# Eight experts of one layer: loop written out, the next expert's transposes ahead of the last product, rows added at evacuation, the inner norm derived from the outer

## The chip, the cores and the metric

The kernel runs on one core of a Trainium2 chip. The metric is the device time of one execution in microseconds (us). TensorE (PE) does the matrix products and the transposes, VectorE (DVE) and ScalarE (ACT) read its results out of PSUM, GpSimd (POOL) does small things in SBUF, and SyncE (SP) issues the DMA transfers. The profile keeps TensorE's weight loads (PEld) apart from its matmuls (PE); they overlap, and since every matmul here has a weight load of its own, the start of a weight load shows when its matmul could be issued.

## The reference

A four-layer network over x of 16 x 256 x 256 (f32). Each layer adds a gated attention and a gated feed-forward part. The change lies in the feed-forward part of the third layer (index 2), which gets the layer norm of x and not x itself:

```python
def _layernorm(x, axis=-1, eps=1e-05): ...          # the outer norm, ahead of every part
def _L2_ffn_ref(x, ln_g, ln_b, attn_w, attn_b, gate_w, w1, b1, w2, b2, next_w, next_b):
    ...
    x_attn = _layernorm(x_flat, ln_g, ln_b) @ attn_w + attn_b + x_flat   # a second, inner norm
    ...
    g = x_attn.reshape(MICRO_BATCHES, E, tpe, Dx)                        # 2 x 8 x 256 x 256
    h = gelu(einsum('metd,edf->metf', g, w1) + b1)                       # 256 -> 1024
    y = einsum('metf,efd->metd', h, w2) + b2                             # 1024 -> 256
    out = gelu(y @ next_w + next_b)
    return out
x = x + tanh(g_ffn[2]) * _L2_ffn_ref(_layernorm(x), ...)
```

Expert e works on batch rows e and e + 8, whatever the gate says.

## The kernel before

The program is a row of stages with a barrier between them; `layer2_experts` is the eighth of nine. It runs eight experts one after the other. Each expert has two halves u = 0, 1 (batches e and e + 8, 256 rows each), and P = 128, C = 2, D = 256. A half has four PSUM banks of its own: A, H0, H1 and Y. For one half the work is:

- **front**: VectorE takes statistics of x (`ln_stats`), GpSimd makes the reciprocal root (`ln_rstd`: an add and a power), VectorE writes the outer norm `xn` (`ln_apply`); then the same three steps on `xn` give the inner norm `nn`. TensorE transposes `nn` into bank A (`transpose4`, four transposes), ScalarE reads that with gain and bias into `n2T`.
- **attention product** (wa): `n2T` by `wa` into A; the rows `xn` themselves are added in the same accumulation, by eight products of 128 columns of `xn` with the identity over both halves (line 2627). ScalarE reads A with the bias `ba` into `xaT` (line 2587).
- **h**: `xaT` by `w1`, four groups a half that go to H0 and H1 in turn; ScalarE's Gelu into `hT` (line 2594).
- **y**: `hT` by `w2` into Y, then VectorE adds `b2` into `yT` (line 2557).
- **z**: `yT` by `wn` into A again; VectorE adds `bn` (line 2562), ScalarE's Gelu, VectorE adds the result times the gate to x (line 2567).

TensorE's order in one expert is wa for both halves, h, y, z, and last the transposes of the next expert (`front(e + 1)`). VectorE makes the next expert's front between its two `yT`: the half u = 0 is read, then the whole front, then u = 1. Those orders are written by hand; the engines meet through counting semaphores. The experts stand in a hardware loop of three rounds with two experts each (`passes`), and the last two experts are written out behind it.

SP's queue loads weights of 2 MB for an expert in two sets of buffers; the set of expert e + 2 is sent for when both `yT` of expert e are read. The first expert's set and `wa`, `wn`, `bn` and the small columns are sent for when the stage begins.

An f32 product of the program is two rows in the profile (64 rows of h an expert for 32 products), a transpose is one.

Of the kernel before, what the change touches and what calls it, by code (L numbers as in the profile page):

```python
# [2454 lines left out]
def layer2_experts(nc, env, w, sem_):  # L2455

    E, F = 8, 1024
    FC = F // P  # L2460
    with ExitStack() as ctx:
# [5 lines left out]
        xn, nn, n2T, xaT, yT, z = (sb(n, [P, 2, C, D]) for n in ("xn", "nn", "n2T", "xaT", "yT", "z"))  # L2467
        hT = sb("hT", [P, 2, FC, S])
        st, mv, rstd = sb("st", [P, 2, C, 6]), sb("mv", [P, 2, C, 2]), sb("rstd", [P, 2, C])
        e_in = [sem_(f"e2_in{k}") for k in range(2)]  # L2470
        (w_in, st_rdy, rstd_rdy, nn_rdy, nT_mm, nT_rdy, xa_mm, xa_rdy, h_mm, h_rdy, y_mm, y_rdy, z_mm, z_rdy, zg_rdy,
         v_ch, f_ch, g_ch) = (
            sem_("e2_" + n) for n in ("w_in", "st_rdy", "rstd_rdy", "nn_rdy", "nT_mm", "nT_rdy", "xa_mm", "xa_rdy",
                                      "h_mm", "h_rdy", "y_mm", "y_rdy", "z_mm", "z_rdy", "zg_rdy", "v_ch", "f_ch",
                                      "g_ch"))

        A, H0, H1, Y = ([env.bank(4 * u + j) for u in (0, 1)] for j in range(4))
        gain_in, a_in = (sem_("e2_" + n) for n in ("gain_in", "wa_in"))
        loads = 2
        block = ctx.enter_context(nc.Block())  # L2480

        def experts(eng, body):

            def two(i, more):
                body(2 * i, True, 0)
                body(2 * i + 1, more, 1)
            passes(eng, two, E // 2)

        @block.sync
        def _(sp):  # L2490
# [7 lines left out]
            def load(e, k):
                at = bass.ds(e, 1)
                sp.dma_start(w1[:, k], w["L2_ffn_w1"][at].rearrange("e (k p) f -> p (e k) f", p=P)).then_inc(e_in[k], 16)  # L2500
                sp.dma_start(w2[:, k], w["L2_ffn_w2"][at].rearrange("e (k p) f -> p (e k) f", p=P)).then_inc(e_in[k], 16)
                sp.dma_start(b1[:, k], b1v[at].rearrange("e p f -> p (e f)")).then_inc(e_in[k], 16)
                sp.dma_start(b2[:, k], b2v[at].rearrange("e p f -> p (e f)")).then_inc(e_in[k], 16)

            load(0, 0)
            load_weight(sp, wn[:], w["L2_ffn_next_w"], w_in)
            sp.dma_start(bn[:], rows(w["L2_ffn_next_b"])).then_inc(w_in, 16)
            load(1, 1)
            with sp.Fori(1, E // 2) as i:
                for k in range(2):  # L2510

                    sp.wait_ge(y_rdy, 4 * i + 2 * k - 2)
                    load(2 * i + k, k)

        @block.gpsimd
        def _(g):
            ch = Chain(g, g_ch)

            def front(e):
                ch.start(4 * e)  # L2520
                for n in range(4):
                    u = n % 2
                    g.wait_ge(st_rdy, 4 * e + n + 1)
                    ln_rstd(g, ch, mv[:, u], rstd[:, u], env.mhalf, env.eps5).then_inc(rstd_rdy, 1)
            front(0)

            def body(e, more, k):
                if more:
                    front(e + 1)
            experts(g, body)  # L2530

        @block.vector
        def _(v):
            ch, fch = Chain(v, v_ch), Chain(v, f_ch)

            def front(e):
                fch.start(6 * e)
                for u in (0, 1):
                    ln_stats(v, fch, env.x[:, e + E * u], st[:, u], mv[:, u], env.scrap).then_inc(st_rdy, 1)
                for u in (0, 1):  # L2540
                    v.wait_ge(rstd_rdy, 4 * e + u + 1)
                    fch.link(ln_apply(v, xn[:, u], env.x[:, e + E * u], mv[:, u], rstd[:, u]))
                    ln_stats(v, fch, xn[:, u], st[:, u], mv[:, u], env.scrap).then_inc(st_rdy, 1)
                for u in (0, 1):
                    v.wait_ge(rstd_rdy, 4 * e + u + 3)
                    ln_apply(v, nn[:, u], xn[:, u], mv[:, u], rstd[:, u]).then_inc(nn_rdy, 1)

            front(0)
            v.wait_ge(w_in, 16 * loads)

            def body(e, more, k):
                for u in (0, 1):
                    if u == 1 and more:
                        front(e + 1)
                    v.wait_ge(y_mm, nth(e, u))
                    for c in range(C):
                        last = v.tensor_scalar(yT[:, u, c], Y[u][:, c], b2[:, k, c:c + 1], None, ALU.add)  # L2557
                    last.then_inc(y_rdy, 1)
                for u in (0, 1):
                    v.wait_ge(z_mm, nth(e, u))  # L2560
                    for c in range(C):
                        last = v.tensor_tensor(z[:, u, c], A[u][:, c], bn[:], ALU.add)
                    last.then_inc(z_rdy, 1)
                for u in (0, 1):
                    v.wait_ge(zg_rdy, nth(e, u))
                    b = e + E * u
                    v.scalar_tensor_tensor(env.x[:, b], z[:, u], env.tg[:, 6:7], env.x[:, b], ALU.mult, ALU.add)
            experts(v, body)

        @block.scalar  # L2570
        def _(a):
            def front(e):
                for u in (0, 1):
                    a.wait_ge(nT_mm, nth(e, u))
                    for c in range(C):
                        last = a.activation(n2T[:, u, c], A[u][:, c], ACT.Identity, scale=gain[:, c:c + 1],
                                            bias=bias[:, c:c + 1])
                    last.then_inc(nT_rdy, 1)
# [3 lines left out]

            def body(e, more, k):
                for u in (0, 1):
                    a.wait_ge(xa_mm, nth(e, u))
                    for c in range(C):
                        last = a.activation(xaT[:, u, c], A[u][:, c], ACT.Identity, bias=ba[:, c:c + 1])
                    last.then_inc(xa_rdy, 1)
                for q in range(FC // C):
                    for u in (0, 1):  # L2590
                        a.wait_ge(h_mm, 8 * e + 2 * q + u + 1)
                        for c in range(C):
                            f = C * q + c
                            last = a.activation(hT[:, u, f], (H0, H1)[q % 2][u][:, c], ACT.Gelu, bias=b1[:, k, f:f + 1])
                        last.then_inc(h_rdy, 1)
                for u in (0, 1):
                    a.wait_ge(z_rdy, nth(e, u))
                    a.activation(z[:, u], z[:, u], ACT.Gelu).then_inc(zg_rdy, 1)
                if more:
                    front(e + 1)  # L2600
            experts(a, body)

        @block.tensor
        def _(pe):
            def front(e):
                for u in (0, 1):
                    pe.wait_ge(nn_rdy, nth(e, u))

                    if not (isinstance(e, int) and e == 0):
                        pe.wait_ge(z_rdy, nth(e - 1, u))  # L2610
                    transpose4(pe, A[u], nn[:, u], env.ident[:]).then_inc(nT_mm, 1)
# [3 lines left out]

            def body(e, more, k):

                pe.wait_ge(e_in[k], 32 * (e - k) + 64)
                for u in (0, 1):
                    pe.wait_ge(nT_rdy, nth(e, u))  # L2620
                    for m in range(C):
                        for kk in range(C):
                            pe.matmul(A[u][:, m], wa[:, kk, chunk(m)], n2T[:, u, kk], start=(kk == 0), stop=False,
                                      skip_group_check=True)
# [4 lines left out]
                    last.then_inc(xa_mm, 1)  # L2629
                for q in range(FC // C):  # L2630
                    for u in (0, 1):
                        if q == 0:
                            pe.wait_ge(xa_rdy, nth(e, u))
                        if q >= 2:

                            pe.wait_ge(h_rdy, 8 * e + 2 * (q - 2) + u + 1)
                        for c in range(C):
                            for kk in range(C):
                                last = pe.matmul((H0, H1)[q % 2][u][:, c], w1[:, k, kk, chunk(C * q + c)],
                                                 xaT[:, u, kk], start=(kk == 0), stop=(kk == C - 1))  # L2640
                        last.then_inc(h_mm, 1)
                for u in (0, 1):
                    pe.wait_ge(h_rdy, 8 * e + 6 + u + 1)
                    product(pe, lambda m: Y[u][:, m], lambda f, m: w2[:, k, f, chunk(m)], lambda f: hT[:, u, f],
                            K=FC).then_inc(y_mm, 1)
                pe.wait_ge(w_in, 16 * loads)
                for u in (0, 1):
                    pe.wait_ge(y_rdy, nth(e, u))
                    product(pe, lambda m: A[u][:, m], lambda kk, m: yT[:, u, kk, chunk(m)],
                            lambda kk: wn[:, kk]).then_inc(z_mm, 1)  # L2650
                if more:
                    front(e + 1)
            experts(pe, body)

# [786 lines left out]
```

## Time and profile before

| | us |
|---|---|
| runs of the kernel before | 2900.1, 2896.9, 2907.57 (median 2900.1) |
| the profiled execution | 2907.57, its span 2905.7 |
| TensorE matmul busy | 2682.1 (92%) |
| VectorE busy | 1584.7 (55%) |
| ScalarE busy | 1292.9 (44%) |
| GpSimd busy | 709.2 (24%) |
| this stage, first statistics to the last row added | 2044.35 to 2376.04, so 331.7 (11%) |

The mean granted clock of TensorE is 0.959 of its full speed. "Granted clock 1.00" is the level of 2.4 GHz, 0.50 that of 1.2 GHz. The profiled execution is the slowest of the three, 7.5 us above the median.

### The profile page before, as it was taken

How to read it: one execution, taken by the hardware profiler on the slowest of the kernel's cores; microseconds unless marked ns; L12 is line 12 of the kernel's file. 1: busy time of each engine (PE TensorE's matmuls, PEld its weight loads, DVE VectorE, ACT ScalarE, POOL GpSimd, SP SyncE). 2: the span in 40 equal slices, each digit the busy share in tenths (PEclk: the TensorE clock that was granted, in tenths of full speed). 3: DMA queues.
4: the chain of work that ended last, by engine and by line, in shares of the span. 5: the costliest groups of instructions: out<-in, count | busy, mean ns of one | idle time of the engine just before them, and what ended most of it. 6: DMA issues, size and time to landing. Idle time of an engine off the chain costs nothing. (4 is left out here: it accounts for less than half of the span.)

```text
span 2905.7 us, 64340 instructions
## 1 busy us (share of the span) xinstructions
PE 2682.1 (92%) x24765; PEld 2044.8 (70%) x24766; DVE 1584.7 (55%) x4380; ACT 1292.9 (44%) x2444; POOL 709.2 (24%) x1095
## 2 busy tenths in 40 slices
PE   7979999999997998997989589999799989969998
PEld 5855555555555887886878455555688878859998
DVE  4747777777771113887766367776232238751111
ACT  1236777676762212553426356665233324532221
POOL 1202333233221000111646423230111015551111
PEclk9999999999997999998899789999899999979999
DMA  9710000000003443931125300100211120035553
GB/s 321 293 35 3 3 3 3 3 3 3 3 3 114 147 157 124 358 126 61 61 81 163 123 24 26 33 18 3 97 53 34 58 81 1 23 133 178 179 180 118
DMA packets 136290, 249.29 MB, mean 86 GB/s; under 512 B 26716, under 2 KB 86364, under 8 KB 129632
## 3 DMA queue, kind: packets, MB, share of 16 engines
q1 hardware_dynamic: 114608, 185.11, 19.1%
q10 hardware_dynamic: 11536, 35.28, 3.1%
q0 software_dynamic: 9888, 25.38, 2.4%
q8 instruction: 172, 2.82, 0.4%
q14 instruction: 86, 0.70, 0.1%
HBM read 148.75 MB, written 97.75 MB: 85 GB/s over the span
## 5 line engine op out<-in xcount | busy, mean ns | idle before, releaser
L532 DVE TENSOR_REDUCE m0hnm<-banks 128x4 f32<-128x1024 f32 x256 | 313.5, 1225 | 157.1 <-PE banks L482 157.1
L553 ACT ACTIVATE m0hpT<-banks 128x1024 f32<-128x1024 f32 x256 | 262.3, 1025 | 181.8 <-PE banks L496 181.6
L482 PE MATMUL banks<-m0hk,m0hq 32*128 32x256 f32 x2048 | 290.6, 401 | 9.5 <-DVE m0hnm L532 8.4
L496 PE MATMUL banks<-m0hq,m0hk 32*128 32x256 f32 x2048 | 291.7, 401 | 1.4 <-ACT m0hpT L553 1.4
L482 PEld LDWEIGHTS banks<-m0hk,m0hq 32*128 32x128 f32 x2048 | 175.2, 184 | 98.4 <-DVE m0hnm L532 89.9
L556 ACT ACTIVATE a2hpT<-banks,A2low 128x512 f32<-128x512 f32 x256 | 162.1, 684 | 128.7 <-PE banks L496 128.7
L532 DVE TENSOR_REDUCE a2hnm<-banks 128x4 f32<-128x1024 f32 x128 | 156.8, 1225 | 99.4 <-PE banks L482 99.3
L496 PEld LDWEIGHTS banks<-m0hq,m0hk 32*128 32x128 f32 x2048 | 182.0, 185 | 3.4 <-issue 1.6
L482 PE MATMUL banks<-a2hk,a2hq 32*128 32x256 f32 x1024 | 148.2, 407 | 9.5 <-DVE a2hnm L532 8.2
L496 PE MATMUL banks<-a2hq,a2hk 32*128 32x256 f32 x1024 | 148.2, 406 | 1.9 <-ACT a2hpT L556 1.9
L3275 PEld LDWEIGHTS banks<-E3xT,E3w 128*128 128x128 f32 x1248 | 146.6, 193 | 2.4 <-DVE E3xT L3199 0.5
L3275 PE MATMUL banks<-E3xT,E3w 128*128 128x128 f32 x1248 | 147.0, 277 | 0.1
L599 POOL TENSOR_TENSOR m0hnrm<-m0hraw,m0hrec 128x256 f32<-128x256 f32 x64 | 39.8, 622 | 436.1 <-DVE m0hrec L594 436.1
L3241 ACT ACTIVATE E3hT<-banks 128x512 f32<-128x512 f32 x78 | 46.6, 598 | 220.8 <-PE banks L3275 212.4
L3286 PE MATMUL banks<-wide_all,E3hT 128*128 x624 | 141.0, 379 | 0.0
L509 PE MATMUL banks<-m0hpT,m0hv 128*32 128x256 f32 x2048 | 136.6, 385 | 1.1 <-ACT m0hpT L553 1.1
L1263 DVE SCALAR_TENSOR_TENSOR x_all<-banks,pick_w,x_all 128x512 f32 (+1 forms) x32 | 24.0, 751 | 206.8 <-PE banks L1226 206.8
L482 PEld LDWEIGHTS banks<-a2hk,a2hq 32*128 32x128 f32 x1024 | 90.0, 187 | 65.1 <-DVE a2hnm L532 49.7
L2557 DVE TENSOR_SCALAR E2yT<-banks,E2b 128x256 f32<-128x256 f32 x32 | 14.0, 477 | 223.2 <-PE banks L61 223.2
L1218 PE MATMUL banks<-wide_all,E0w 128*128 (+1 forms) x512 | 117.3, 383 | 9.8 <-DMA E0w<-in_L_ffn_fw_dram 9.8
L3286 PEld LDWEIGHTS banks<-wide_all,E3hT 128*128 128x128 f32 x624 | 115.6, 190 | 14.2
L1226 PE MATMUL banks<-E0w,E0hT 128*128 128x256 f32 x512 | 115.6, 379 | 0.0
(493 smaller groups left out, 6157.4 us busy)
## 6 DMA issues: line engine op xcount, KB each, us to landing
E3w<-in_L_ffn_W_dram SPq DMA_DIRECT2D x39, 1024.0 KB, 4.8
slots<-A0pad SPq DMA_DIRECT2D x8, 4290.0 KB, 33.7
slots_x<-A1pad ACTq DMA_DIRECT2D x8, 4290.0 KB, 13.8
E0w<-in_L_ffn_fw_dram SPq DMA_DIRECT2D x64, 512.0 KB
E2w<-in_L_ffn_w_dram SPq DMA_DIRECT2D x16, 1024.0 KB
E1xin<-slots SPq DMA_DIRECT2D x71, 130.0 KB
m0hq<-m0hnmT SPq DMA_DIRECT2D x512, 1.0 KB
A2routed<-routed SPq DMA_DIRECT2D x16, 512.0 KB, 3.8
```

Source lines behind the costliest of these rows:

```text
L482: ins = pe.matmul(self.scores[:, j, tc], self.q[self.strip(half, j), u, e, c, chunk(tc)], self.k[self.strip(half, j), u, e, c], start=True ...
L496: ins = pe.matmul(self.turned[:, j, kc], self.k[self.strip(half, j), u, e, c, chunk(kc)], self.q[self.strip(half, j), u, e, c], start=True ...
L509: ins = pe.matmul(self.out[32 * g:32 * g + 32, e], self.v[:, u, kc, 8 * c + 2 * g + e], self.pT[:, e, g, kc], start=(kc == 0), stop=(kc == ...
L532: v.tensor_reduce(self.nm[:, n % 2, :, 16 * half:16 * half + 9:8].rearrange("p c g -> p g c"), self.scores, AX.X, ALU.max, negate=True).th ...
L553: ins = a.activation(dst, self.turned, ACT.Exp)
L556: ins = a.activation(dst[:, :, kc], self.turned[:, :, kc], ACT.Exp, bias=self.low[:, n // 4, kc:kc + 1])
L599: g.tensor_tensor(self.nrm[:].rearrange("p s e k -> p e s k"), self.raw[:, :, :, 0:KD], self.rec[:].unsqueeze(3).broadcast_to([P, 2, 8, KD ...
L1218: last = pe.matmul(env.bank(4 * (j % 2) + half)[:, m], w1[:, j, k, chunk(f)], env.n2T[:, 2 * i + j // 2, k], start=(k == 0), stop=(k == C ...
L1226: last = pe.matmul(env.bank(4 * (j % 2) + 2)[:, tc], hT[:, j % 2, k, chunk(tc)], w2[:, j, k], start=(k == 0), stop=(k == FC - 1))
L3241: a.activation(hT[:, u, 4 * q:4 * q + 4], hidden_bank(u, q), ACT.Gelu).then_inc(h_free, 1)
L3275: last = pe.matmul(hidden_bank(u, q)[:, c], w1[:, u, k, chunk(4 * q + c)], xT[:, u, k], start=(k == 0), stop=(k == C - 1))
L3286: last = pe.matmul(bank(6 + u)[:, 0], hT[:, u, f], w2[:, e, f].rearrange("p e d -> p (e d)"), start=(f == 0), stop=(f == FC - 1))
```

## The change

Only `layer2_experts` changes. The loop is gone: the eight experts are written out for all engines. The semaphores are counted with constants.

```diff
         @block.gpsimd
...
-            def front(e):
-                ch.start(4 * e)
-                for n in range(4):
-                    u = n % 2
-                    g.wait_ge(st_rdy, 4 * e + n + 1)
-                    ln_rstd(g, ch, mv[:, u], rstd[:, u], env.mhalf, env.eps5).then_inc(rstd_rdy, 1)
...
+            for e in range(E):
+                for u in (0, 1):
+                    g.wait_ge(st_rdy, 2 * e + u + 1)
+                    g.tensor_scalar(var[:, u, 1], mv[:, u, :, 1], 1.0 + 1e-5, 1e-10, ALU.mult, ALU.add)
+                    ch.link(g.tensor_tensor(var[:, u, 0], mv[:, u, :, 1], env.eps5[:], ALU.add))
+                    g.tensor_tensor(root[:, u].rearrange("p t c -> p (t c)"), var[:, u].rearrange("p t c -> p (t c)"),
+                                    env.mhalf[:, 0:2 * C], ALU.pow).then_inc(rstd_rdy, 1)
         @block.vector
...
+                for u in (0, 1):
+                    v.wait_ge(rstd_rdy, 2 * e + u + 1)
...
+                    for t, dst in ((0, xn), (1, nn)):
+                        for c in range(C):
+                            ins = v.tensor_scalar(dst[:, u, c, :], env.x[:, e + E * u, c, :], mv[:, u, c, 0:1],
+                                                  root[:, u, t, c:c + 1], ALU.subtract, ALU.mult)
+                    ins.then_inc(nn_rdy, 1)
...
-                for u in (0, 1):
-                    if u == 1 and more:
-                        front(e + 1)
-                    v.wait_ge(y_mm, nth(e, u))
...
+            for e in range(E):
+                for u in (0, 1):
+                    v.wait_ge(xa_mm, 2 * e + u + 1)
+                    v.tensor_tensor(xaT[:, u], A[u], xT[:, u], ALU.add).then_inc(xa_rdy, 1)
+                if e:
+                    residual(e - 1)
+                if e + 1 < E:
+                    front(e + 1)
+                for u in (0, 1):
+                    v.wait_ge(y_mm, 2 * e + u + 1)
...
         @block.scalar
...
+                    for c in range(C):
+                        a.activation(n2T[:, u, c], H0[u][:, c], ACT.Identity, scale=gain[:, c:c + 1], bias=bias[:, c:c + 1])
+                    for c in range(C):
+                        ins = a.activation(xT[:, u, c], H1[u][:, c], ACT.Identity, bias=ba[:, c:c + 1])
+                    ins.then_inc(nT_rdy, 1)
...
         @block.tensor
...
-                    transpose4(pe, A[u], nn[:, u], env.ident[:]).then_inc(nT_mm, 1)
+                    transpose4(pe, H0[u], nn[:, u], env.ident[:])
+                    transpose4(pe, H1[u], xn[:, u], env.ident[:]).then_inc(nT_mm, 1)
...
-                pe.wait_ge(e_in[k], 32 * (e - k) + 64)
...
-                        for tc in range(C):
-
-                            last = pe.matmul(A[u][:, m, chunk(tc)], xn[:, u, tc, chunk(m)], env.ident[:],
-                                             start=False, stop=True, skip_group_check=True)
...
+                    pe.wait_ge(nT_rdy, 2 * e + u + 1)
+                    if e:
+                        pe.wait_ge(z_rdy, 2 * e - 2 + u + 1)
+                    product(pe, lambda m: A[u][:, m], lambda kk, m: wa[:, kk, chunk(m)], lambda kk: n2T[:, u, kk])\
+                        .then_inc(xa_mm, 1)
+                pe.wait_ge(e_in[k], 64 * (e // 2 + 1))
...
+                if e + 1 < E:
+                    front(e + 1)
                 pe.wait_ge(w_in, 16 * loads)
```

In words: the inner norm is no longer taken from statistics of `xn`; its root is worked out from the variance of x, and `nn` is written straight from x beside `xn`. The rows `xn` are transposed too, read by ScalarE with the bias into a new tile `xT`, and added by VectorE when it reads the attention product. The transposes go to H0 and H1 and not to A. The wait for the expert's own weights stands ahead of h and no longer ahead of wa. VectorE makes the next front ahead of both `yT`, behind the reading of the attention product and the former expert's last addition to x.

TensorE's order of one expert before, where it is written out behind the loop (E2nn and E2xn are the two norms, E2n2T the transposed inner norm, E2xaT, E2hT and E2yT the inputs of h, y and z):

```order
L77 MATMUL banks<-ident,E2nn 128x128 x8
L2623 MATMUL banks<-E2n2T,E2wa 128x256 x2
L2627 MATMUL banks<-ident,E2xn 128x128 x2
L2623 MATMUL banks<-E2n2T,E2wa 128x256 x2
...
L2639 MATMUL banks<-E2xaT,E2w 128x256 x32
L61 MATMUL banks<-E2hT,E2w 128x256 x32
L61 MATMUL banks<-E2wn,E2yT 128x256 x8
```

The same stretch of TensorE's order in the changed kernel, from the wa of one expert to that of the next:

```order
L61 MATMUL banks<-E2n2T,E2wa 128x256 x8
L61 MATMUL banks<-E2xaT,E2w 128x256 x32
L61 MATMUL banks<-E2hT,E2w 128x256 x32
L77 MATMUL banks<-ident,E2nn 128x128 x4
L77 MATMUL banks<-ident,E2xn 128x128 x4
L77 MATMUL banks<-ident,E2nn 128x128 x4
L77 MATMUL banks<-ident,E2xn 128x128 x4
L61 MATMUL banks<-E2wn,E2yT 128x256 x8
L61 MATMUL banks<-E2n2T,E2wa 128x256 x8
```

The sixteen transposes stand between y and z, and the products with the identity are gone. On VectorE the order of one expert before, from the first `yT` to the addition to x (written out behind the loop; E2st and E2mv are the statistics):

```order
L2557 TENSOR_SCALAR E2yT<-banks,E2b 128x256 x2
L84 BN_STATS E2st<-x_all 128x6 x2
...
L101 TENSOR_SCALAR E2xn<-x_all,E2mv,E2rstd 128x256 x2
L84 BN_STATS E2st<-E2xn 128x6 x2
...
L101 TENSOR_SCALAR E2nn<-E2xn,E2mv,E2rstd 128x256 x4
L2557 TENSOR_SCALAR E2yT<-banks,E2b 128x256 x2
L2562 TENSOR_TENSOR E2z<-banks,E2bn 128x256 x4
L2567 SCALAR_TENSOR_TENSOR x_all<-E2z,tg,x_all 128x512 x2
```

VectorE in the changed kernel, one expert in the middle:

```order
L2550 TENSOR_TENSOR E2xaT<-banks,E2xT 128x512 x2
L2544 SCALAR_TENSOR_TENSOR x_all<-E2z,tg,x_all 128x512 x2
L2524 BN_STATS E2st<-x_all 128x6 x2
...
L2536 TENSOR_SCALAR E2xn<-x_all,E2mv,E2root 128x256 x2
L2536 TENSOR_SCALAR E2nn<-x_all,E2mv,E2root 128x256 x2
...
L2558 TENSOR_SCALAR E2yT<-banks,E2b 128x256 x4
L2565 TENSOR_TENSOR E2z<-banks,E2bn 128x256 x4
```

The front stands ahead of the pair of `yT` and no longer inside it, and the reading of the attention product, ScalarE's before, is VectorE's.

## Rows read from the trace of the kernel before

The stretches of rows 1 and 7 give length, then busy time (and instructions) of PE, PEld, DVE, ACT and POOL, then the granted clock, the DMA engines' busy share and GB/s.

**Rows 1.** Stretches by engine: steady experts, then the stage's opening.
```profile
2063.05:2342.44 279.39, 265.29 (x1291) 230.59 (x1289) 76.84 (x266) 86.77 (x187) 26.87 (x56) 1.00 0.14 45
2044.30:2063.05 18.75, 10.33 (x40) 8.51 (x40) 6.58 (x28) 4.16 (x7) 3.85 (x8) 0.56 0.76 261
```

**Rows 2.** What weight loads waited for, 2063 to 2376: us, times, longest.
```profile
PEld banks L61 <- DVE E2yT L2557: 7.0, 7, 1.0
PEld banks L2623 <- issue: 5.8, 5, 1.2
PEld banks L77 <- issue: 5.0, 7, 0.7
PEld banks L2623 <- ACT E2n2T L2576: 2.2, 2, 1.1
```

**Rows 3.** Weight loads in time: start, us, line, names [idle before, releaser]; several experts.
```profile
2097.75 0.73 PEld L2623 LDWEIGHTS banks<-E2n2T,E2wa 128*128 128x128 f32 x4 [1.15 <-issue]
...
2102.98 13.69 PEld L2639 LDWEIGHTS banks<-E2xaT,E2w 128*128 128x128 f32 x64
...
2130.51 1.70 PEld L61 LDWEIGHTS banks<-E2wn,E2yT 128*128 128x128 f32 x8
2133.20 1.59 PEld L61 LDWEIGHTS banks<-E2wn,E2yT 128*128 128x128 f32 x8 [0.99 <-DVE E2yT L2557]
2134.82 0.57 PEld L77 LDWEIGHTS banks<-ident,E2nn 128*128 128x128 f32 x4
2136.11 0.42 PEld L77 LDWEIGHTS banks<-ident,E2nn 128*128 128x128 f32 x4 [0.71 <-issue]
2137.61 0.73 PEld L2623 LDWEIGHTS banks<-E2n2T,E2wa 128*128 128x128 f32 x4 [1.09 <-ACT E2n2T L2576]
...
2337.21 0.73 PEld L2623 LDWEIGHTS banks<-E2n2T,E2wa 128*128 128x128 f32 x4 [1.15 <-issue]
```

**Rows 4.** VectorE and ScalarE in time, the turn from expert 1 to 2.
```profile
2124.01 0.88 DVE L2557 TENSOR_SCALAR E2yT<-banks,E2b 128x256 f32<-128x256 f32 x2 [26.38 <-PE banks L61]
2124.81 0.74 DVE L84 BATCH_NORM_STATS2 E2st<-x_all 128x6 f32 x2
...
2132.28 0.87 DVE L2557 TENSOR_SCALAR E2yT<-banks,E2b 128x256 f32<-128x256 f32 x2
...
2135.24 0.76 DVE L2562 TENSOR_TENSOR E2z<-banks,E2bn 128x256 f32<-128x256 f32 x2 [1.42 <-PE banks L61]
...
2136.56 1.92 ACT L2576 ACTIVATE E2n2T<-banks,E2bias,E2gain 128x256 f32<-128x256 f32 x4
```

**Rows 5.** Groups by line and form: out<-in xcount | busy us, mean ns | idle.
```profile
L2962 DVE TENSOR_TENSOR A3on<-banks,A3den 128x512 f32<-128x512 f32 x16 | 11.0, 688 | 3.6 <-PE banks L3065 2.6 <-issue 0.8
L2587 ACT ACTIVATE E2xaT<-banks,E2ba 128x256 f32<-128x256 f32 x32 | 13.4, 471 | 31.7 <-PE banks L2627 31.7
L101 DVE TENSOR_SCALAR E2nn<-E2xn,E2mv,E2rstd 128x256 f32<-128x256 f32 x32 | 11.5, 402 | 4.7 <-POOL E2rstd L96 4.7
L722 POOL TENSOR_TENSOR M0root<-M0var,mhalf 128x4 f32<-128x4 f32 x16 | 16.5, 1033 | 1.2
L720 POOL TENSOR_SCALAR M0var<-M0mv 128x2 f32<-128x2 f32 x16 | 3.1, 193 | 14.8 <-DVE M0mv L782 14.6
```

**Rows 6.** All engines in time, the stage's opening.
```profile
2044.35 0.75 DVE L84 BATCH_NORM_STATS2 E2st<-x_all 128x6 f32<-128x256 f32 x2 [1.31 <-PEq L3348]
...
2050.66 0.72 PEld L77 LDWEIGHTS banks<-ident,E2nn 128*128 128x128 f32 x4 [9.37 <-DVE E2nn L101]
...
2054.95 2.07 PE L2623 MATMUL banks<-E2n2T,E2wa 128*128 128x256 f32 x4 [1.85 <-DMA E2b<-in_L_ffn_b_dram]
```

**Rows 7.** Short stretches: the clock's rise here and in the next stage.
```profile
2060.50:2061.00 0.50, 0.50 (x3) 0.38 (x3) 0.00 (x0) 0.50 (x2) 0.00 (x0) 0.64 1.09 320
2385.00:2386.00 1.00, 1.00 (x5) 0.85 (x5) 0.35 (x2) 0.00 (x0) 0.92 (x2) 0.94 0.64 205
```

**Rows 8.** The next stage's first product on TensorE, in time.
```profile
2382.03 3.06 PEld L61 LDWEIGHTS banks<-A3wq,a3xnT 128*128 128x128 f32 x8 [1.15 <-issue]
```

More of the change, by code:

```diff
@@ L2496, in _, with load @@
             b2v = w["L2_ffn_b2"].rearrange("p (e c) -> e p c", e=E)
[L2498 to L2505, printed above, removed]
+            def load(e):
+                k = e % 2
+                sp.dma_start(w1[:, k], w["L2_ffn_w1"][e].rearrange("(k p) f -> p k f", p=P)).then_inc(e_in[k], 16)
+                sp.dma_start(w2[:, k], w["L2_ffn_w2"][e].rearrange("(k p) f -> p k f", p=P)).then_inc(e_in[k], 16)
+                sp.dma_start(b1[:, k], b1v[e]).then_inc(e_in[k], 16)
+                sp.dma_start(b2[:, k], b2v[e]).then_inc(e_in[k], 16)
+            load(0)
             load_weight(sp, wn[:], w["L2_ffn_next_w"], w_in)
             sp.dma_start(bn[:], rows(w["L2_ffn_next_b"])).then_inc(w_in, 16)
[L2508 to L2513, printed above, removed]
+            load(1)
+            for e in range(2, E):
+                sp.wait_ge(y_rdy, 2 * e - 2)
+                load(e)
         @block.gpsimd
@@ L2556, in body @@
                     for c in range(C):
-                        last = v.tensor_scalar(yT[:, u, c], Y[u][:, c], b2[:, k, c:c + 1], None, ALU.add)
-                    last.then_inc(y_rdy, 1)
+                        ins = v.tensor_scalar(yT[:, u, c], Y[u][:, c], b2[:, e % 2, c:c + 1], None, ALU.add)
+                    ins.then_inc(y_rdy, 1)
+                if e == 0:
+                    v.wait_ge(w_in, 16 * loads)
                 for u in (0, 1):
-                    v.wait_ge(z_mm, nth(e, u))
+                    v.wait_ge(z_mm, 2 * e + u + 1)
@@ L2561, in body @@
                     for c in range(C):
-                        last = v.tensor_tensor(z[:, u, c], A[u][:, c], bn[:], ALU.add)
-                    last.then_inc(z_rdy, 1)
-                for u in (0, 1):
[L2565 to L2568, printed above, removed]
+                        ins = v.tensor_tensor(z[:, u, c], A[u][:, c], bn[:], ALU.add)
@@ L2570, in _ @@
+                    ins.then_inc(z_rdy, 1)
+            residual(E - 1)
         @block.scalar
@@ L2573, in front @@
                 for u in (0, 1):
-                    a.wait_ge(nT_mm, nth(e, u))
+                    a.wait_ge(nT_mm, 2 * e + u + 1)
                     for c in range(C):
-                        last = a.activation(n2T[:, u, c], A[u][:, c], ACT.Identity, scale=gain[:, c:c + 1],
-                                            bias=bias[:, c:c + 1])
-                    last.then_inc(nT_rdy, 1)
+                        a.activation(n2T[:, u, c], H0[u][:, c], ACT.Identity, scale=gain[:, c:c + 1], bias=bias[:, c:c + 1])
+                    for c in range(C):
+                        ins = a.activation(xT[:, u, c], H1[u][:, c], ACT.Identity, bias=ba[:, c:c + 1])
+                    ins.then_inc(nT_rdy, 1)
             a.wait_ge(gain_in, 16 * 3)
             front(0)
[L2583 to L2588, printed above, removed]
+            a.wait_ge(e_in[0], 64)
+            for e in range(E):
+                if e:
+                    a.wait_ge(e_in[e % 2], 64 * (e // 2 + 1))
                 for q in range(FC // C):
@@ L2593, in body @@
                             f = C * q + c
-                            last = a.activation(hT[:, u, f], (H0, H1)[q % 2][u][:, c], ACT.Gelu, bias=b1[:, k, f:f + 1])
-                        last.then_inc(h_rdy, 1)
+                            ins = a.activation(hT[:, u, f], (H0, H1)[q % 2][u][:, c], ACT.Gelu, bias=b1[:, e % 2, f:f + 1])
+                        ins.then_inc(h_rdy, 1)
+                if e + 1 < E:
+                    front(e + 1)
                 for u in (0, 1):
-                    a.wait_ge(z_rdy, nth(e, u))
+                    a.wait_ge(z_rdy, 2 * e + u + 1)
                     a.activation(z[:, u], z[:, u], ACT.Gelu).then_inc(zg_rdy, 1)
-                if more:
-                    front(e + 1)
-            experts(a, body)
         @block.tensor
@@ L2632, in body @@
                         if q == 0:
-                            pe.wait_ge(xa_rdy, nth(e, u))
+                            pe.wait_ge(xa_rdy, 2 * e + u + 1)
                         if q >= 2:
                             pe.wait_ge(h_rdy, 8 * e + 2 * (q - 2) + u + 1)
[L2637 to L2641, printed above, removed]
+                        product(pe, lambda m: (H0, H1)[q % 2][u][:, m], lambda kk, m: w1[:, k, kk, chunk(C * q + m)],
+                                lambda kk: xaT[:, u, kk]).then_inc(h_mm, 1)
                 for u in (0, 1):
@@ L2645, in body @@
                             K=FC).then_inc(y_mm, 1)
+                if e + 1 < E:
+                    front(e + 1)
                 pe.wait_ge(w_in, 16 * loads)
                 for u in (0, 1):
[L2648 to L2653, printed above, removed]
+                    pe.wait_ge(y_rdy, 2 * e + u + 1)
+                    product(pe, lambda m: A[u][:, m], lambda kk, m: yT[:, u, kk, chunk(m)], lambda kk: wn[:, kk])\
+                        .then_inc(z_mm, 1)
 def layer3(nc, env, w, sem_):
```

59 lines of the change are left out of this document (23 added, 36 removed).

## The prediction

> **What bounds the kernel now.** I looked first at busy time by stretches. In the steady experts TensorE's matmuls are busy 265.3 of 279.4 us at a granted clock of 1.00, VectorE and ScalarE under a third [rows 1]: the stage is TensorE's, and only what TensorE does or waits for counts. The opening is another regime, 18.75 us at a mean clock of 0.56 [rows 1].
>
> Then the waits of the weight loads. They sat idle 7.0 us for the second `yT`, 8.0 us (5.8 + 2.2) ahead of wa and 5.0 us ahead of the second half's transposes [rows 2]. That is 20.0 us over seven turns from one expert to the next, 2.86 each. The waits called "issue" are the same waits as the named one: they stand at the same places with the same length [rows 3].
>
> Then the turn in time. From wa of expert 1 (2097.75) to wa of expert 7 (2337.21) are six turns, so a turn is 239.46 / 6 = 39.91 us [rows 3]. Inside it h and y take 2130.51 - 2102.98 = 27.53 us for 128 rows, 0.215 us each. z and wa have 16 rows each, 3.44 us. From wa's start to h's start are 2102.98 - 2097.75 = 5.23 us, so the identity products take 5.23 - 3.44 = 1.79 us. What is left for the eight transposes is 39.91 - 27.53 - 3.44 - 5.23 - 2.86 = 0.85 us, 0.106 each; the four that directly follow z spread over 0.57 us, 0.143 each [rows 3], which I keep as an upper bound.
>
> Last, why it waits. VectorE reads `yT` of half 0 at 2124.01, starts the front at 2124.81 and reads half 1 only at 2132.28, 7.47 us later, though y had ended by 2130.51 [rows 3, 4]. So the second z starts late, and the transposes, which share bank A with z, wait for VectorE to read that z at 2135.24; then wa waits for ScalarE's reading of the transposes, from 2136.56 on [rows 3, 4]. Three engines pass one thing round with TensorE empty in between.
>
> **The change, part by part.**
>
> *Order of the turn.* The transposes need nothing of z now, and the front is long done when y ends. After y TensorE has 16 transposes, 1.70 us, then z, 3.44 us, then wa. I put y's end at 0 and count an engine's start 0.45 us after the last weight load of its product (the second z's loads end at 2133.20 + 1.59 = 2134.79, VectorE starts at 2135.24) [rows 3, 4]. Second `yT`: ready at 0.45 + 0.87 = 1.3, needed at 1.7 + 1.7 = 3.4. ScalarE's four readings of a half take 2 x 0.48 + 2 x 0.47 = 1.9 us [rows 4, 5]; half 0 is ready at 0.85 + 0.45 + 1.9 = 3.2 and half 1 at 5.1, needed at 5.1 and 6.9. The second z is read 0.45 + 0.76 = 1.2 us after its last load, and wa's second half comes 1.72 later: 0.5 us to spare. All three waits go, 2.86 us a turn.
>
> *Rows added at evacuation.* The identity products go: 1.79 us a turn. Eight transposes come: 0.85 (up to 1.14). VectorE's addition of 128x512 from PSUM is not in this trace; the nearest rows are 0.69 us for such a product of two operands and 0.76 for a pair of additions with the same number of elements [rows 4, 5]. Each half is ready 1.14 to 1.21 us after its wa and h of that half comes 1.72 after it. It costs nothing, with 0.5 us of cover; were the cover gone, all of h would wait for it and each further us would be a us a turn.
>
> *Inner norm from the variance.* VectorE loses two statistics a turn. GpSimd's power over 128x4 takes 1.03 us and the extra scalar step 0.19, as the same trick does elsewhere in this kernel [rows 5]; both lie in the front. That now runs during h: behind the second addition and the two updates of x. Even at its old 7.47 us plus some 3 us ahead of it, it ends 11 us into h and y's 27.5. VectorE's new wait there, for the former expert's Gelu, holds the front and through it the transposes; it has more than 15 us of cover. Nothing in the steady turn.
>
> *Weights.* The wait for an expert's weights stands later, the transfers are sent for a little earlier in the turn, since `yT` is read earlier. No cost, no gain in the turn.
>
> *Loop written out.* The turn into expert 2 crosses the loop's end and wa waits 1.09 us there; the turn into expert 7 lies in straight code, 1.15 [rows 3]. So the branch costs nothing today. The Trainium skill (Runtime: NRT & Kernel Launch, Instruction fetch mechanics) says that a taken branch out of the prefetched pages stalls for a fetch, by which written-out code would gain more than my sum; the trace does not show it here.
>
> So a turn saves 2.86 + 1.79 - 0.85 = 3.80 us (3.5 with the dear transposes, all sixteen at 0.143: 3.2), and seven turns 26.6 (22.4).
>
> *Opening.* Before: statistics from 2044.35, first transposes at 2050.66, first product at 2054.95, held for the last small weight of expert 0 [rows 6]. After: two statistics (0.95 with their aggregation, by the 0.75 of the row and an estimate of 0.2), GpSimd 0.19 + 0.19 + 1.03 with small gaps, 1.5, four applications at 0.40 [rows 5, 6]: transposes at about 2048.5. Eight of them at the half clock, 0.18 to 0.21 us each by the 0.72 us of four [rows 6], 0.45 for the hand-over, four readings: first wa at about 2052.7, without the wait for the weights. Those arrive at 2054.95 and h needs them later. The clock was full 2060.86 - 2054.95 = 5.9 us after the first product (the 0.64 of that half us puts the step at 2060.86) [rows 6, 7], and in the next stage 2385.12 - 2382.03 = 3.1 us after it [rows 7, 8]. wa then ends, and h starts, between 2057.8 and 2059.1, at the latest 2059.6 if all of wa runs at half speed (16 rows at 0.43). Before, h started where wa's 16 + 16 rows ended, 27.53 + 7.15 us (z 3.44, transposes 0.85, idle 2.86) ahead of the next expert's wa at 2097.75: 2063.07. I take 2058.6, so 4.5 us saved (3.5 to 5.3).
>
> **Sum.** 26.6 + 4.5 = 31.1 us. The stage's end is as before: the last expert has no next front, and y, z and the additions to x follow each other as they did. On the profiled execution 2907.6 - 31.1 = 2876.5. That one is 7.5 us above the median of its three runs, and nothing says this stage is why; against the median, 2900.1 - 31.1 = 2869.
>
> **The rivals.**
>
> *New waits take part of it.* Two hand-overs have only 0.5 us of cover: z read before wa, and the sums before h. If VectorE's two steps are each 1 to 1.5 us longer than their rows, each costs 0.5 to 1 us, so 1 to 2 us a turn and 7 to 14 us in all: 2876 to 2883. Against it: both are VectorE alone, which is otherwise idle at that time. 12 in 100.
>
> *The clock drops in the turn: slower.* Sixteen transposes stand in a row where products with full columns stood nearby before. If the granted clock falls to 0.50 there and stays low through transposes, z and wa, those 8.6 us become 17.2, 60 us in seven turns, net 29 slower: 2929. It decides from 4.4 us lost per turn, half of that stretch. Against it: TensorE was emptier in today's turn (2.86 us idle and eight transposes) and kept 1.00 throughout [rows 1, 2]. The Trainium skill speaks for this rival (TensorE: Matmul & The Clock Gate, PE-mode transpose): there the full clock does not engage for transposes. The trace agrees for the opening, where eight transposes alone left it at the lower level, and does not in the turn. 4 in 100.
>
> *The change does not do what it says.* The stage gets shorter and the next one gives it back, because its start waits for something else. Its first work is VectorE's statistics of x, which follow this stage's last addition, so I see nothing else: 4 in 100, about 2900.
>
> *More.* The turn saves the same, the opening 7 or more and the next stage's clock rises earlier: 35 to 40, 2860 to 2865; 6 in 100.
>
> **How the numbers follow.** The forecast holds 74 in 100: 2869, with 27 to 33 us saved, and some 4 us either way for the spread of single runs (2896.9 to 2907.6): 2863 to 2877. The range reaches into the first rival and the last one: 2861 to 2882. A measurement of this kernel can tell about 0.5%, 14.5 us, from no change. The forecast, "more" and nearly all of "new waits" lie beyond it: 0.91 faster; 0.05 the same; 0.04 slower.
>
> **What would show it.** In the profile after: a turn of 36.1 us from wa to wa; no idle row of weight loads between y and the next h; sixteen transposes in about 1.7 us; h of expert 0 starting 14 to 15 us into the stage instead of 18.7; a granted clock of 1.00 from there to the last z. I am wrong if weight loads still wait on VectorE's sums or on z, if the transposes take over 0.15 us each, or if the clock dips in the turn.

## The result, and the profile after

The changed kernel takes 2864.1 us (median of 4 runs), the kernel before 2901.1 beside it: ratio 0.9878, interval 0.9858 to 0.9898. A second measurement gave 2867.6 us (6 runs) against 2898.4 (10 runs): 0.9887, interval 0.9863 to 0.9911. So the change saves 36.9 us by the first, 30.7 by the second. The profiled execution took 2864.39 us with a span of 2862.2.

A cleaner measure is the stage itself, from its first statistics of x to the next stage's first statistics: 332.64 us before, 300.78 after, so **31.9 us**. Both intervals hold it (29.6 to 41.2 us, and 25.8 to 39.7). Of the two executions of experiment 6 below, one took 9042.8 us, more than three times any other, and is left out.

Stretches of the profile after, with columns as in [rows 1]; the first answers to the steady experts there, the second to the opening, the last two to [rows 7]:

```profile
2043.88:2319.00 275.12, 275.12 (x1331) 243.32 (x1330) 74.30 (x212) 87.47 (x199) 19.65 (x42) 1.00 0.16 53
2031.71:2043.88 12.17, 7.72 (x32) 6.71 (x33) 5.33 (x19) 3.39 (x8) 2.82 (x6) 0.61 0.84 255
2041.00:2041.50 0.50, 0.50 (x3) 0.39 (x2) 0.00 (x0) 0.33 (x1) 0.00 (x0) 0.68 1.16 307
2041.50:2042.00 0.50, 0.50 (x4) 0.45 (x3) 0.00 (x0) 0.00 (x0) 0.00 (x0) 1.00 1.21 297
```

TensorE's matmuls are busy all of the steady stretch where 14 us were empty before, and the opening is 12.2 us long and not 18.7. What weight loads waited for in the whole stage (2031 to 2333), as in [rows 2], is two waits of the opening and no more:

```profile
PEld banks L77 <- DVE E2nn L2536: 7.2, 1, 7.2
PEld banks L61 <- issue: 0.7, 1, 0.7
```

A turn in time, weight loads, VectorE and ScalarE (they answer to [rows 3, 4]; L77 transposes, L61 is every product, L2558 yT, L2565 z, L2550 the new addition):

```profile
2057.69 13.79 PEld L61 LDWEIGHTS banks<-E2hT,E2w 128*128 128x128 f32 x64
2071.50 0.57 PEld L77 LDWEIGHTS banks<-ident,E2nn 128*128 128x128 f32 x4
2072.05 0.47 PEld L77 LDWEIGHTS banks<-ident,E2xn 128*128 128x128 f32 x4
...
2073.36 3.32 PEld L61 LDWEIGHTS banks<-E2wn,E2yT 128*128 128x128 f32 x16
2076.71 3.43 PEld L61 LDWEIGHTS banks<-E2n2T,E2wa 128*128 128x128 f32 x16
...
2071.92 0.88 DVE L2558 TENSOR_SCALAR E2yT<-banks,E2b 128x256 f32<-128x256 f32 x2 [6.03 <-PE banks L61]
2075.47 0.76 DVE L2565 TENSOR_TENSOR E2z<-banks,E2bn 128x256 f32<-128x256 f32 x2 [2.67 <-PE banks L61]
2077.12 0.76 DVE L2565 TENSOR_TENSOR E2z<-banks,E2bn 128x256 f32<-128x256 f32 x2 [0.90 <-PE banks L61]
2078.85 0.69 DVE L2550 TENSOR_TENSOR E2xaT<-banks,E2xT 128x512 f32<-128x512 f32 x1 [0.97 <-PE banks L61]
2080.57 0.69 DVE L2550 TENSOR_TENSOR E2xaT<-banks,E2xT 128x512 f32<-128x512 f32 x1 [1.04 <-PE banks L61]
...
2072.79 1.02 ACT L2575 ACTIVATE E2n2T<-banks,E2bias,E2gain 128x256 f32<-128x256 f32 x2 [13.85 <-PE banks L77]
```

From one h to the next (2043.88 to 2080.16) are 36.28 us: h 13.81, y 13.81, sixteen transposes 1.86 (2071.50 to 2073.36), z 3.35, wa 3.45. No weight load carries an idle time any more; it is VectorE and ScalarE that wait for TensorE. Seven turns are alike to 0.01 us.

The opening in time (answers to [rows 6]; the power's price to [rows 5]):

```profile
2031.71 0.75 DVE L2524 BATCH_NORM_STATS2 E2st<-x_all 128x6 f32<-128x256 f32 x2 [1.29 <-PEq L3330]
2033.37 1.02 POOL L2512 TENSOR_TENSOR E2root<-E2var,mhalf 128x4 f32<-128x4 f32 x1
2035.86 0.71 PEld L77 LDWEIGHTS banks<-ident,E2nn 128*128 128x128 f32 x4 [7.21 <-DVE E2nn L2536]
2039.80 4.05 PEld L61 LDWEIGHTS banks<-E2n2T,E2wa 128*128 128x128 f32 x16 [0.66 <-issue]
2043.88 2.13 PEld L61 LDWEIGHTS banks<-E2xaT,E2w 128*128 128x128 f32 x10
2332.49 0.75 DVE L203 BATCH_NORM_STATS2 a3st<-x_all 128x6 f32<-128x256 f32 x2 [0.94 <-PEq L3330]
```

Transposes 4.15 us into the stage, wa at 8.09, h at 12.17. The clock is full from 2041.32 (the 0.68 of its half us), 1.5 us after the first product. The last row is the next stage's start; from there to the end of the span are 529.7 us, 528.7 before; the twelve profiles, whatever the kernel, have 528.6 to 530.8 there, so no giving back shows.

### The profile page after: what moved, and what is told of

It reads as the page before. It is cut to its first block and busy times, and to the rows that moved or that the text cites. A ratio compares the mean times of both kernels' runs of the same rounds, so it can differ in the third digit from the quotient of the medians.

```text
span 2862.2 us, 63825 instructions
## 1 busy us (share of the span) xinstructions
PE 2660.0 (93%) x24701; PEld 2032.0 (71%) x24702; DVE 1580.4 (55%) x4316; ACT 1285.0 (45%) x2439; POOL 701.0 (24%) x1079
## 5 line engine op out<-in xcount | busy, mean ns | idle before, releaser
L1249 ACT ACTIVATE E0hT<-banks 128x512 f32<-128x512 f32 x64 | 34.7, 594 | 179.3 <-PE banks L1218 179.3
```

## The experiments

Each kernel's stage in its profile, and its time. Opening: stage's start to the first weight load of h; turn: h to h.

| kernel | stage | opening | turn | median | ratio to before, interval |
|---|---|---|---|---|---|
| before | 332.64 | 18.70 | 39.87 to 39.93 | 2901.1 | |
| 1 loop written out | 332.74 | 18.55 | 39.93 to 40.01 | 2898.0 | 0.9999, 0.9983 to 1.0016 |
| 2 and the order | 313.65 | 18.73 | 37.20 | 2877.5 | 0.9916, 0.9896 to 0.9937 |
| 4 changed, statistics of the rows | 302.22 | 13.60 | 36.28 | 2866.5 | 0.9885, 0.9866 to 0.9904 |
| changed | 300.78 | 12.17 | 36.28 | 2864.1 | 0.9878, 0.9858 to 0.9898 |
| 3 changed, transposes behind z | 309.38 | 12.16 | 37.51 | 2879.3 | 0.9934, 0.9911 to 0.9958 |
| 5 changed, front between yT | 301.07 | 12.46 | 36.28 | 2863.9 | 0.9867, 0.9847 to 0.9887 |
| 6 changed, transposes twice | 315.03 | 14.20 | 38.03 | one run, 2882.5 | |
| 7 changed, addition twice | 301.05 | 12.53 | 36.28 | 2870.1 | 0.9888, 0.9868 to 0.9908 |
| 8 changed, products ahead | 299.16 | 10.55 | 36.28 | 2862.0 | 0.9860, 0.9843 to 0.9876 |
| 9 changed, again | 300.84 | 12.23 | 36.28 | 2867.6 | 0.9887, 0.9863 to 0.9911 |
| 10 before, again | 332.61 | 18.67 | 39.86 to 39.94 | 2900.4 | |

The stage of one kernel repeats to 0.06 us (9 and 10), the whole kernel to some ten us, so most verdicts below rest on the stage. Differences of 0.3 us between kernels are not to be read as an effect: in 5 and 7 the clock rose 0.6 us later than in the changed kernel, at 10.2 us into the stage and not 9.6, and 0.6 us more at half speed is 0.3 us of work.

**1. The loop written out, alone** (kernel before; SP's loop of loads, not shown, too).

```diff
-            def two(i, more):
-                body(2 * i, True, 0)
-                body(2 * i + 1, more, 1)
-            passes(eng, two, E // 2)
+            for e in range(E):
+                body(e, e + 1 < E, e % 2)
...
```

> The kernel before with its loop of experts written out and nothing else. Lengths of the stage are from its first statistics to the first statistics of the next stage: 332.6 us before, 300.8 after. My theory: the loop cost nothing, since the turn over the loop's end was as long as one in straight code; stage 332.6 us, turn 39.9, time as before within 5 us. Rival, written-out code is what pays: a stage of 325 us or less.

Turn and stage stay. The waits of [rows 3] are all there in straight code, the third of them 1.16 where it was 1.09 at the loop's end:

```profile
2122.11 1.59 PEld L61 LDWEIGHTS banks<-E2wn,E2yT 128*128 128x128 f32 x8 [1.00 <-DVE E2yT L2553]
...
2125.01 0.42 PEld L77 LDWEIGHTS banks<-ident,E2nn 128*128 128x128 f32 x4 [0.71 <-issue]
2126.59 0.73 PEld L2619 LDWEIGHTS banks<-E2n2T,E2wa 128*128 128x128 f32 x4 [1.16 <-issue]
```

The loop cost nothing: 0.9999. The Trainium skill (Runtime: NRT & Kernel Launch, Instruction fetch mechanics) says that a taken branch to code outside the prefetched pages stalls; no run here shows such a stall.

**2. The order, on top of 1.** Transposes go to H0, `front(e + 1)` stands ahead of z on TensorE and ahead of both yT on VectorE, and ScalarE reads the transposes ahead of its last Gelu; identity products and statistics of the rows stay.

```diff
+                if more:
+                    v.wait_ge(xa_mm, 2 * e + 2)
+                    front(e + 1)
                 for u in (0, 1):
-                    if u == 1 and more:
-                        front(e + 1)
...
-                    transpose4(pe, A[u], nn[:, u], env.ident[:]).then_inc(nT_mm, 1)
+                    transpose4(pe, H0[u], nn[:, u], env.ident[:]).then_inc(nT_mm, 1)
...
+                if more:
+                    front(e + 1)
                 pe.wait_ge(w_in, 16 * loads)
...
```

> The kernel before, written out, with the order of the turn alone: transposes (eight, of the inner norm only) into the other bank and ahead of the last product, VectorE's front ahead of both readings of y, ScalarE's reading of the transposes ahead of its last Gelu. Rows still added by products with the identity, inner norm still from statistics, the wait for the weights still ahead of the attention product. My theory: the order gives the three waits of a turn, 2.8 us: turn 37.1, stage 332.6 - 7 x 2.8 = 313 us, opening as before (18.7 us). Rival, the order needs the shorter front or the added rows to pay: a turn of 38.5 or more, stage 323 or more.

The turn falls by 2.71 us, the stage by 19.1: the three waits (2.86 by the weight loads' idle time), of which none is left in the turns, and 60% of the whole gain. The opening is untouched, its first product still waits and then runs at half speed until 16.6 us into the stage (the 0.83 of its quarter us). Weight loads in time, the last two rows one turn apart, then that stretch:

```profile
2043.64 0.71 PEld L77 LDWEIGHTS banks<-ident,E2nn 128*128 128x128 f32 x4 [0.60 <-DVE E2nn L101]
2046.58 1.35 PEld L2619 LDWEIGHTS banks<-E2n2T,E2wa 128*128 128x128 f32 x4 [2.22 <-issue]
...
2054.74 5.27 PEld L2635 LDWEIGHTS banks<-E2xaT,E2w 128*128 128x128 f32 x25
...
2091.93 12.17 PEld L2635 LDWEIGHTS banks<-E2xaT,E2w 128*128 128x128 f32 x57
```

```profile
2052.51:2052.76 0.25, 0.25 (x2) 0.21 (x2) 0.00 (x0) 0.25 (x2) 0.00 (x0) 0.83 0.93 240
```

**3. The changed kernel with the transposes behind z again.**

```diff
-                if e + 1 < E:
-                    front(e + 1)
                 pe.wait_ge(w_in, 16 * loads)
...
+                if e + 1 < E:
+                    front(e + 1)
```

> The changed kernel with the sixteen transposes put back behind the last product; all else as changed. My theory: the attention product must then wait for ScalarE to read the first half's transposes (0.45 + 1.9 us after eight of them, while the other eight take 0.93): about 1.4 to 1.6 us more a turn, turn 37.8, stage 311 to 312 us. Rival, with other banks and an early front the place no longer matters: stage 301.

The direction is right, the size a little less: 1.23 us a turn. One wait came back, ahead of wa for ScalarE's reading of the transposes, in all seven turns:

```profile
PEld banks L61 <- ACT E2xT L2577: 8.4, 7, 1.2
```

So the place ahead of z is worth 8.6 us of the stage even with the front early and A kept free. z is the work that covers ScalarE.

**4. The changed kernel with the inner norm from statistics of the rows**, as before the change.

```diff
-                    ch.link(g.tensor_tensor(var[:, u, 0], mv[:, u, :, 1], env.eps5[:], ALU.add))
...
+                    ln_rstd(g, ch, mv[:, u], rstd[:, u], env.mhalf, env.eps5).then_inc(rstd_rdy, 1)
...
+                    fch.link(ln_apply(v, xn[:, u], env.x[:, e + E * u], mv[:, u], rstd[:, u]))
+                    ln_stats(v, fch, xn[:, u], st[:, u], mv[:, u], env.scrap).then_inc(st_rdy, 1)
...
+                    ln_apply(v, nn[:, u], xn[:, u], mv[:, u], rstd[:, u]).then_inc(nn_rdy, 1)
```

> The changed kernel with the inner norm taken again from statistics of the outer one. My theory: the front is hidden under the products, so the turn stays at 36.3 us and only the opening grows, by 2 to 2.5 us; stage 303 us. Rival, the shorter front is what lets the transposes come early: a turn longer by 1 us or more, stage 310 or more.

Nothing in the turn, 1.4 us in the opening where 2 to 2.5 were expected (1.1 against the 12.46 of experiment 5, whose clock rose later). The transposes begin 2.17 us later, but part of that is won back: the clock is full before the first product is issued, so wa takes 3.34 us and not 4.08. Weight loads in time, then stretches of half a us:

```profile
2040.52 0.71 PEld L77 LDWEIGHTS banks<-ident,E2nn 128*128 128x128 f32 x4 [9.37 <-DVE E2nn L101]
...
2042.92 0.87 PEld L77 LDWEIGHTS banks<-ident,E2xn 128*128 128x128 f32 x4
2044.46 3.32 PEld L61 LDWEIGHTS banks<-E2n2T,E2wa 128*128 128x128 f32 x16 [0.67 <-issue]
2047.80 2.35 PEld L61 LDWEIGHTS banks<-E2xaT,E2w 128*128 128x128 f32 x11
```

```profile
2043.50:2044.00 0.50, 0.50 (x4) 0.29 (x2) 0.00 (x0) 0.50 (x3) 0.00 (x0) 0.52 1.19 303
2044.00:2044.50 0.50, 0.17 (x2) 0.04 (x1) 0.00 (x0) 0.50 (x2) 0.00 (x0) 1.00 1.08 318
```

What TensorE did in this stage before the clock rose (at about 2044, 3.5 us after the first weight load) is sixteen transposes in a row and nothing else.

**5. The changed kernel with VectorE's front between the two yT again.**

```diff
-                if e + 1 < E:
-                    front(e + 1)
                 for u in (0, 1):
+                    if u == 1 and e + 1 < E:
+                        front(e + 1)
```

> The changed kernel with VectorE's next front put back between the two readings of y; transposes still ahead of the last product. In the changed kernel the front takes 5.7 us and its first half is ready 4.1 us after it starts. My theory: it starts about 5.6 us before y ends, so both halves are ready when TensorE comes to them, and the second reading of y has the transposes and half the last product as cover; turn 36.3 to 36.6 us, stage 301 to 303. Rival, the early front is what removed the wait for the second reading of y: turn 37 or more, stage 306 or more.

The turn is the same, and the 0.3 us of the stage are the clock's later rise in the opening (the last row below). The shorter front ends just ahead of the second y, VectorE then waits 0.40 us and reads yT as early as before:

```profile
2062.16 0.88 DVE L2558 TENSOR_SCALAR E2yT<-banks,E2b 128x256 f32<-128x256 f32 x2 [20.03 <-PE banks L61]
...
2067.94 0.73 DVE L2536 TENSOR_SCALAR E2nn<-x_all,E2mv,E2root 128x256 f32<-128x256 f32 x2
2069.07 0.88 DVE L2558 TENSOR_SCALAR E2yT<-banks,E2b 128x256 f32<-128x256 f32 x2 [0.40 <-PE banks L61]
```

```profile
2038.57:2038.82 0.25, 0.25 (x2) 0.25 (x1) 0.00 (x0) 0.00 (x0) 0.00 (x0) 0.60 0.96 283
```

So with the short inner norm the front's new place is not needed; with the long one (7.47 us, [rows 4]) it was in the way. Either edit removes this wait.

**6. The changed kernel with every transpose made twice**, 32 in a turn.

```diff
                     transpose4(pe, H0[u], nn[:, u], env.ident[:])
+                    transpose4(pe, H1[u], xn[:, u], env.ident[:])
+                    transpose4(pe, H0[u], nn[:, u], env.ident[:])
                     transpose4(pe, H1[u], xn[:, u], env.ident[:]).then_inc(nT_mm, 1)
```

> The changed kernel with every set of transposes done twice into the same banks (32 an expert for 16); the result is the same. My theory: the full clock holds and sixteen more transposes cost 0.116 us each: 1.9 us a turn, turn 38.1, granted clock 1.00 in all turns; opening 1 to 3 us longer; stage 315 to 317 us. Rival, transposes let the clock fall: a clock under 1.00 in the turns and a turn of 42 us or more, stage 340 or more.

Sixteen more cost 1.75 us a turn, 0.109 each, and the clock stays full through all 32. Weight loads of a turn, then the stretch they lie in, and last the clock's rise in the opening:

```profile
2077.86 0.58 PEld L77 LDWEIGHTS banks<-ident,E2nn 128*128 128x128 f32 x4
...
2081.03 0.47 PEld L77 LDWEIGHTS banks<-ident,E2xn 128*128 128x128 f32 x4
2081.46 3.32 PEld L61 LDWEIGHTS banks<-E2wn,E2yT 128*128 128x128 f32 x16
```

```profile
2078.00:2084.00 6.00, 6.00 (x46) 5.64 (x45) 1.31 (x4) 3.49 (x8) 0.00 (x0) 1.00 0.57 205
2046.04:2046.29 0.25, 0.25 (x4) 0.25 (x2) 0.00 (x0) 0.00 (x0) 0.00 (x0) 0.83 0.89 279
```

In the opening the 32 transposes start 4.15 us into the stage and wa at 10.47; the clock is full from 10.09, again with transposes alone before it, but 5.9 us after the first of them and not 3.5.

**7. The changed kernel with VectorE's addition made twice.**

```diff
+                    v.tensor_tensor(hT[:, u, 0:C], A[u], xT[:, u], ALU.add)
                     v.tensor_tensor(xaT[:, u], A[u], xT[:, u], ALU.add).then_inc(xa_rdy, 1)
```

> The changed kernel with VectorE's addition of the rows done twice (first into another tile that is overwritten later), which doubles its 0.69 us; the result is the same. My theory: each half had about 0.5 us of cover, so of 0.66 us more only 0.1 to 0.2 show: turn 36.4 to 36.7 us, stage 301.5 to 304. Rival, the addition is on the path already: 0.66 us for a half, so turn 36.9 to 37.6, stage 305.5 or more.

The turn did not move, against 0.1 to 0.2 expected. The second addition ends at 2084.82, the weight loads of h begin at 2084.94:

```profile
2083.53 0.69 DVE L2550 TENSOR_TENSOR E2hT<-banks,E2xT 128x512 f32<-128x512 f32 x1 [0.97 <-PE banks L61]
2084.14 0.68 DVE L2551 TENSOR_TENSOR E2xaT<-banks,E2xT 128x512 f32<-128x512 f32 x1
...
2081.39 3.43 PEld L61 LDWEIGHTS banks<-E2n2T,E2wa 128*128 128x128 f32 x16
2084.94 3.12 PEld L61 LDWEIGHTS banks<-E2xaT,E2w 128*128 128x128 f32 x15
```

From wa to h are 3.55 us instead of 3.45, but h is as much shorter up to y: the cover of 0.6 us is used up to its last tenth.

**8. The changed kernel with nine products of the identity with itself ahead of the first transposes.**

```diff
+            for n in range(9):
+                pe.matmul(Y[0][:, 0, 0:P], env.ident[:], env.ident[:], start=True, stop=True)
             front(0)
```

> The changed kernel with nine products of the identity with itself, into a bank not yet used, while TensorE waits for the first front; nothing else. The changed kernel's opening takes 12.17 us from the first statistics to h, with the clock at 0.50 until 9.6 us. My theory: TensorE busy from the stage's start brings the full clock earlier, at about 4 to 7 us, so transposes and attention product of the first expert run faster; opening 10 to 11 us, stage 298.5 to 300 us, time 1 to 2 us less than the changed kernel. Rival, the clock does not answer to these products, or they hold up the transposes: opening 12.2 us or more, stage 301 or more.

They run while VectorE and GpSimd make the first front, and the clock is full at about 2038.4, 2.8 us into the stage where 4 to 7 were expected, ahead of the transposes. Weight loads in time, then the stretch of the rise:

```profile
2035.51 3.43 PEld L2608 LDWEIGHTS banks<-ident 128*128 128x128 f32 x18 [3.02 <-issue]
2039.69 0.42 PEld L77 LDWEIGHTS banks<-ident,E2nn 128*128 128x128 f32 x4 [0.74 <-DVE E2nn L2536]
...
2042.75 3.32 PEld L61 LDWEIGHTS banks<-E2n2T,E2wa 128*128 128x128 f32 x16 [0.57 <-issue]
2046.09 4.08 PEld L61 LDWEIGHTS banks<-E2xaT,E2w 128*128 128x128 f32 x19
```

```profile
2038.00:2039.00 1.00, 1.00 (x9) 0.94 (x7) 0.75 (x3) 0.00 (x0) 0.77 (x4) 0.81 0.82 248
```

The stage is 1.6 us shorter than the changed kernel's; the times, 2862.0 and 2864.1, cannot tell that.

**9 and 10. Both kernels once more, unaltered.**

> The changed kernel once more, unaltered. Theory: the stage itself takes 300.8 us with turns of 36.28, as before, and the stage of this change explains 31.9 us of the difference of the medians; what a ratio shows beyond that (36.9 us by the medians so far) comes from single executions, in which the unchanged experts of the second layer took 292 to 304 us whatever the kernel. By it the ratio over five rounds is 0.987 to 0.990. Rival: the written-out stage also shortens an unchanged one, the attention of the third layer just ahead of it, which took 377.9 to 379.6 us in all seven profiles with the whole change's structure and 382.1 to 384.1 in the three with before's front. By it this profile shows 377.9 to 379.6 again, and a ratio of 0.986 to 0.988.

> The kernel before once more, unaltered. Theory (the stages ahead vary by chance): its stage takes 332.6 us with turns of 39.9; the attention of the third layer, ahead of it, anywhere from 378 to 384 us. Rival (that stage is shorter in the changed kernels, run after run): 382 to 384 us again.

The stages came out as before, to 0.06 us. The unchanged attention of the third layer took 382.0 us in both, so the rival of 9 falls as it was put: that stage is not shorter in the changed kernel run after run. A link that shows in most executions is not ruled out (see the end).

## Why the prediction was right, point by point

Forecast 2869 us, measured 2864.1 and 2867.6; 31.1 us saved forecast, 31.9 in the stage.

**Turn.** Forecast 3.80 us saved, measured 39.91 - 36.28 = 3.63. The order gave 2.71 (2 against 1), the rest 0.92: identity products out, eight transposes in (2 against 4). The difference of 0.17 is the transposes: sixteen in 1.86 us and not in 1.70. The first four, next to the product ahead of them, take 0.55, the others 0.44 each. Seven turns: 25.4 us of 26.6.

**Opening, the mis-sized term.** Forecast 4.5 us (3.5 to 5.3), measured 18.70 - 12.17 = 6.5. The start of the transposes was right (4.15 us into the stage, forecast 4.15), and so nearly was the first wa (8.09, forecast 8.35). Wrong was the time from wa to h: 4.1 us and not 5.9, since the clock rose 1.5 us after the first product, where the prediction carried over 3.1 and 5.9 us from two places. At those, TensorE had sat idle for 1.15 and 1.85 us just ahead of the product [rows 8, 6]. Here sixteen transposes stand in a row with 0.66 us idle behind them, and in experiments 4 and 6 the full clock came with nothing but such transposes before it. What sets the moment is not shown: it came 3.5 us after the first transpose in 4, 5.5 in the changed kernel, 5.9 in 6. Five executions with this opening (changed, 3, 5, 7, 9) have the same weight loads up to wa to 0.01 us, and the clock rose between 9.60 and 10.20 us into the stage; so some 0.3 us of the 6.5 are chance.

Most of the opening's gain does not need the shorter inner norm: experiment 4, still with the long norm, has 13.60 against the 18.73 of experiment 2. An estimate of the parts of these 5.1 us: wa starts 0.3 earlier (10.26 and 10.57); from there to h experiment 2 takes 8.16 in the opening and 5.34 in its turn (2086.59 to 2091.93), so the clock is some 2.8; experiment 4 takes 3.34, so the identity products that are gone are some 2.0.

**By parts**, from the stages of the table: loop 0, order 19.1, rows at evacuation (with the clock that comes earlier, and the weights awaited later) 11.4, inner norm 1.4, together 31.9.

**New waits (12 in 100)** did not come; their margin is now measured. VectorE may take 0.6 us more per half ahead of h and costs nothing; the prediction had 0.5. Ahead of wa, z's second half is read by 2077.88 and wa's second half comes at 2076.71 + 1.72 = 2078.43.

**The clock drops (4 in 100)** is wrong: 1.00 through 16 and through 32 transposes. The Trainium skill (TensorE: Matmul & The Clock Gate, PE-mode transpose), which spoke for it, has the full clock not engage for transposes. The trace does not agree, and it decides: the opening of experiment 4 shows 0.52, then 1.00, with sixteen transposes alone before it. The prediction's reading, that eight left the clock at the lower level, holds for those eight alone.

**Gives back (4 in 100)** fell with the 529.7 us behind the stage, within the spread of all profiles. **More (6 in 100)** was half right: the opening went that way, 6.5 of the 7 or more, and the first median of 2864.1 lies in its times, but its 35 us were not saved in the stage.

**The difference of the medians.** Two profiled executions differ by 43.5 us of span, 31.9 of it in the stage. The rest lies in unchanged stages ahead, which differ by 12.6 us, less the 1.0 behind the stage: the second layer's experts took 292 us in one execution and 303 in another of the same kernel (changed 292.2 and 303.3, before 303.0 and 295.6). A saving of 31 us is to be read from the stage.

## What to carry to other kernels

When three engines pass one thing round, look for work of the bound engine that needs none of them, and put the hand-over ahead of it: the order alone gave 19 of 32 us without a single instruction less. Adding rows by products with the identity costs 1.79 us where eight transposes and an addition on an idle engine cost under 1; price both in the time of the engine that bounds. Removing VectorE work in the turn was worth nothing there, and 1.4 us in the one stretch, the opening, where TensorE waits for it.

## What the runs showed of the hardware

Not expected: a row of sixteen f32 transposes of 128x128 was followed by the step of TensorE's granted clock from 0.50 to 1.00 before any product (experiment 4; with 32 in a row, experiment 6), while eight of them, with a gap between and 2.2 us idle behind, were not (experiment 2). During nine f32 products of the identity, 3.4 us of weight loads under other engines' work, it rose as well (experiment 8). Experiments 4, 6 and 8 are one profile each, and the moment of the step varies where the work ahead of it does not.

Open: the third layer's attention, unchanged and ahead of this stage, took 382.0 to 384.1 us in the four profiles built on the kernel before (before twice, 1 and 2), and 377.9 to 379.6 in seven of the eight built on the changed one, 382.0 in the eighth. What sets it was not found; its 2 to 6 us may be part of what the medians show beyond the stage's 31.9.
